# A graph network kernel: attention's software pipeline stretched, and its rings made longer

## The reference, cut to what matters

```python
h = relu(layernorm(x))
for l in range(3):                       # "the layers": mean over neighbours
    agg = segment_sum(h[src], dst) / degree
    h = leaky_relu(agg @ Wl.T + b + h @ Wr.T, 0.01)
x = x + h
h = relu(layernorm(x)) @ W               # "attention"
e = leaky_relu(a_s[src] + a_d[dst], 0.2) # with one more self edge per node
p = exp(e - segment_max(e, dst)[dst])
x = x + segment_sum(h[src] * p, dst) / segment_sum(p, dst) + bias
```

## Time and profile before

| | us |
|---|---|
| median of 3 runs (3214.66 to 3219.05) | 3217.39 |
| profiled execution | 3214.68 |
| its span | 3213.0 |
| PE busy | 2058.8 (64%) |
| DVE busy | 1978.0 (62%) |
| POOL busy | 1840.3 (57%) |
| ACT busy | 1405.6 (44%) |
| mean granted TensorE clock | 0.859 of 2.4 GHz |

### The profile page before, as it was taken

The page is one execution under the profiler, slowest core; times in us unless marked ns, Lnnn a source line. Parts: engine busy times, 40 slices in busy tenths (PEclk is TensorE's granted clock), DMA queues, the critical chain, the costliest instruction groups (busy, mean ns, idle before and its releaser), DMA issues. The chain is left out here.

```text
span 3213.0 us, 51338 instructions
## 1 busy us (share of the span) xinstructions
PE 2058.8 (64%) x12372; PEld 1794.7 (56%) x12372; DVE 1978.0 (62%) x8287; ACT 1405.6 (44%) x3735; POOL 1840.3 (57%) x1800
## 2 busy tenths in 40 slices
PE   0005877778765767777748888988944455445455
PEld 0004766666655656666647777877744444444444
DVE  8984444444444544444538888888846566666666
ACT  4781333333321222222215555555555555555555
POOL 1017666666646666666566666666535555555553
PEclk9997888889887988888869999999977777777778
DMA  6774766667655666666747777778745454445454
GB/s 210 254 254 122 201 194 192 192 191 199 189 161 152 203 194 197 192 190 198 209 127 223 221 225 224 220 220 225 219 124 129 123 128 125 125 124 130 124 129 113
DMA packets 600968, 576.10 MB, mean 179 GB/s; under 512 B 83395, under 2 KB 561301, under 8 KB 600640
## 3 DMA queue, kind: packets, MB, share of 16 engines
q1 hardware_dynamic: 402272, 337.58, 35.8%
q0 software_dynamic: 57280, 105.90, 14.9%
q10 hardware_dynamic: 141120, 129.32, 11.7%
HBM read 378.74 MB, written 207.75 MB: 183 GB/s over the span
## 5 line engine op out<-in xcount | busy, mean ns | idle before, releaser
L619 POOL DMA_INDIRECT rows<-tab,idx x1323 | 1373.2, 1038 | 808.0 <-issue 361.0
L834 PE MATMUL bank<-mask,rows 128*128 128x128 f32 (+1 forms) x3528 | 693.4, 336 | 176.8 <-issue 126.9
L1235 DVE TENSOR_TENSOR sage<-bank,sage 128x256 f32<-128x256 f32 x588 | 247.3, 421 | 835.7 <-remote 527.8
L834 PEld LDWEIGHTS bank<-mask,rows 128*128 128x128 f32 x3528 | 593.7, 211 | 248.0 <-issue 186.4
L619 POOL DMA_INDIRECT rows<-tab_c,idx x441 | 447.2, 1014 | 426.8 <-PE bank L945 177.2
L707 ACT ACTIVATE sage<-bank,b_col 128x256 f32<-128x256 f32 x392 | 185.2, 473 | 772.6 <-remote 462.5
L935 PE MATMUL bank<-ident,mask 128*128 128x128 f32 x784 | 168.5, 353 | 376.3 <-ACT mask L767 347.0
L1215 DVE TENSOR_SCALAR mask<-iota,dcol 128x256 f32<-128x256 f32 (+1 forms) x1323 | 406.2, 339 | 0.1
L935 PEld LDWEIGHTS bank<-ident,mask 128*128 128x128 f32 x784 | 121.6, 184 | 392.7 <-ACT mask L767 358.0
L787 ACT ACTIVATE sage<-cut_w,ed 128x256 f32<-128x256 bf16 (+1 forms) x441 | 184.8, 472 | 301.5 <-DVE ed L1439 289.5
L859 PE MATMUL bank<-sage,wcat 128*128 128x256 f32 x784 | 273.0, 434 | 43.1 <-issue 34.6
(11 more groups left out here) (210 smaller groups left out, 3402.6 us busy)
## 6 DMA issues: line engine op xcount, KB each, us to landing
sage<-inv_d SPq DMA_DIRECT2D x588, 128.0 KB
turned<-sage ACTq DMA_DIRECT2D x392, 128.0 KB
tab<-sage ACTq DMA_DIRECT2D x392, 128.0 KB
sage<-turned SPq DMA_DIRECT2D x392, 128.0 KB
tab_c<-sage ACTq DMA_DIRECT2D x196, 132.0 KB
own_w<-tab_c SPq DMA_DIRECT2D x196, 132.0 KB
tab<-sage SPq DMA_DIRECT2D x49, 512.0 KB, 3.6
xin<-tab SPq DMA_DIRECT2D x196, 128.0 KB
```

The lines of the kernel that those rows point to most:

```text
L619: eng.indirect_dma_start(out=rows[:, s.win[w], 0:width], out_offset=None, in_=table, in_offset=bass.IndirectOffsetOnAxis(ap=idx[:, s.w + w ...
L834: m = eng.matmul(to[:, a:b], rows[:, s.win[w], 0:D], mask[:, s.mw[w], c:c + b - a], start=(w == 1), stop=(w == 2))
L1235: eng.tensor_tensor(agg_t[:, o.r, :], ps[:, 0:TILE], own_t[:, o.v, :], ALU.add).then_inc(S["sum_v"], 1)
```

## The change

All rings counted in twelve tiles are counted in sixteen (`UNROLL`, `DEEP`): `rows` and `cut` hold 36 windows, `own_c` 16 tiles, `ed` and `pself_2` four groups. `DEEP` sets the waits of the gathers in all stages. In attention ACT takes the exponentials of tile s-7, PE the products of tile s-8, DVE the result of tile s-9, and DVE's back part runs two steps after the front part. The own rows' semaphores are one per group in place of one per tile, and DVE waits once per group. The space comes from the general path's tables, which now lie over `mask`.

```diff
-UNROLL = 12
+UNROLL = 16
-DEEP = 12
+DEEP = 16
...
-        low = sb("low", [P, P])
+        spare = mask[:, :, :].rearrange("p r e -> p (r e)")
+        low = spare[:, 0:128]
...
@@ sync, phase_c
-                        eng.dma_start(own_c[:, g.q, :, :], node_rows(tab_c, g.t)).then_inc(S[f"cl{g.q}"], 16)
+                        eng.dma_start(own_c[:, g.q, :, :], node_rows(tab_c, g.t)).then_inc(S[f"cl{g.g}"], 16)
@@ scalar, phase_c
-                o = s.at(-5)
+                o = s.at(-7)
...
-            steps(eng, 5, phase_c)
+            steps(eng, 7, phase_c)
@@ tensor, phase_c
-                o = s.at(-6)
+                o = s.at(-8)
...
-            steps(eng, 6, phase_c)
+            steps(eng, 8, phase_c)
@@ vector
         def fast_vector(eng, op, close_up):
+            eng.wait_ge(S["low_g"], 11)
...
                 if front:
-                    for n in range(SG):
-                        f = s.at(n - SG)
-                        eng.wait_ge(S[f"cl{f.q}"], 16 * (f.uses(DEEP) + 1))
+                    eng.wait_ge(S[f"cl{o.g}"], 16 * SG * (o.uses(DEEP) + 1))
...
-                r = s.at(-7)
+                r = s.at(-9)
...
-                b = s.at(-2)
-                back = b.there and s.k == 1
+                b = s.at(-3)
+                back = b.there and s.k == 2
...
-            steps(eng, 7, phase_c)
+            steps(eng, 9, phase_c)
```

More of the change, by code:

```diff
@@ L315, in build @@
         rden = sb("rden", [P, 2])
-        low = sb("low", [P, P])
+        spare = mask[:, :, :].rearrange("p r e -> p (r e)")
+        low = spare[:, 0:128]
         se = sb("se", [P, 2], I32)
[L320 to L325, removed]
+        g_row = spare[:, 128:260]
+        g_dst = spare[:, 260:392]
+        g_sum = spare[:, 392:524]
+        g_new = spare[:, 524:656]
+        g_node = spare[:, 656:788]
+        g_init = spare[:, 2068:2332].rearrange("p (j c) -> p j c", j=2)
         df = sb("df", [P, 1])
-        wide = sb("wide", [P, P])
-        same = sb("same", [P, P])
-        tmp = sb("tmp", [P, P])
+        wide = spare[:, 788:916]
+        same = spare[:, 916:1044]
+        tmp = spare[:, 1044:1172]
         g1 = sb("g1", [P, 8])
         w_idx = sb("w_idx", [P, 1], I32)
[L332 to L336, removed]
+        g_x = spare[:, 1172:1300]
+        g_x1 = spare[:, 1300:1428]
+        g_x1b = spare[:, 1428:1556]
+        g_h = spare[:, 1556:1684]
+        g_t = spare[:, 1684:1940]
         g_st = sb("g_st", [P, 6])
         g_mv = sb("g_mv", [P, 2])
-        g_out = sb("g_out", [P, D])
+        g_out = spare[:, 1940:2068]
         bank = [ctx.enter_context(nc.psum_tensor(f"bank{i}", [P, 512], F32)) for i in range(8)]
@@ L360, in build @@
                  "st3 x1_v x1b_v stx0 stx1 "
-                 "one_v turn cl0 cl1 cl2 cl3 cl4 cl5 cl6 cl7 cl8 cl9 cl10 cl11 cx0 cx1 cx2 cx3 cx4 cx5 cut_v sc_a zm_done "
+                 "one_v turn cl0 cl1 cl2 cl3 cx0 cx1 cx2 cx3 cx4 cx5 cut_v sc_a zm_done "
                  "mx_v mt_a fs_v pf_a br_done hs_v pr_a t1_v "
```

## The result

The changed kernel takes 3111.72 us, median of 4 runs (3110.88 to 3112.29), against 3218.12 us of the kernel before (4 runs, 3214.66 to 3219.05): a ratio of 0.9668, interval 0.9652 to 0.9684. The forecast was 3107. The profiled execution took 3110.88 us with a span of 3109.2, that is 103.8 us less than before.

A forecast was written before the change was run, and what follows sets the result against it. Attention was held by waits among ACT, DVE and PE, no engine full. From 3214.68 us, 42 x 2.33 = 97.9 and 7 x 2.28 = 16.0 off, 3 added: 3103.8; as a median 3106.5, say 3107, range 3060 to 3150 (chance 0.50).

The forecast's parts named there:

- Rings of sixteen: Gathers, all stages: deeper rings could win at most 43.6 us of PE's and the scores' waits; 0 taken for the layers.
- My own mark: Sign in the three layers: the prediction is wrong if they move by more than 15 us; within 5 us was expected.
- So if the lateness stays, DVE's 4.37 us stay, now at L1417: Attention, DVE's back part: the wait for PE moves from `edge_v` to the next mx, about 4 us a group.
- The ring of waits: Attention: ACT waits for `ed` of DVE (275.0 us), DVE at `edge_v` (163.1), PE for ACT's scores (330.0).
- another mark of mine: Sign in attention: wrong if DVE's mx at L1417 has no wait of about 4 us a group.
- my 14.6: Attention's mean group after the change: 42 groups at 15.13 us and 7 at POOL's floor of 11.7.
- a late group: Attention: one of 42 in 49 groups where DVE waits at L1413; 17.46 us before, 15.13 forecast, 2.33 saved each.
- The end: End of attention: two more tiles' results to make after the last score, about 3 us more, bounds 0 to 6.
- The lateness goes: Rival in attention: PE's late completions vanish or fall beside other work, POOL's 11.7 us is the floor; 2987 us, chance 0.29.
- The lateness grows with what is queued behind the bridge: Rival in attention: PE's release comes 2.5 us later, 17.63 us a group; 3253 us, slower, chance 0.12.
- No gain: Rival in attention: the wait moves whole to L1417, 17.46 us a group stays, 3 us added; 3220 us, chance 0.09.
- The rule on estimated ends: PE in attention: the profiler only estimates a matmul's end, so DVE's 4.37 us of idle time are PE's.

The follow-up runs named there:

- the first experiment: Changed kernel with the gathers of the three layers waiting as if the ring held twelve tiles, attention untouched: 3086.67 us, ratio 0.9596.
- the pipeline alone: Kernel before, rings of twelve kept, with only attention's steps moved to -7, -8, -9 and the back part to -3: 3095.3 us, ratio 0.9623.
- the leads (16, 12, 6): Changed kernel, layers' gathers waiting as for 16, 12 or 6 tiles: 3111.72 us, 3086.67 us; 6 in single layers: first 20 tiles 74.0 (layer 3), 62.0 us (layer 1).
- the pauses: Changed kernel with layers' lead 12, plus two waited-for POOL memsets after each of tiles 4 to 15 in attention: 2700.38 us on the other chip; first group 18.0 us in a mixed run.
- The additional raise: Changed kernel with layers' lead 12, plus one more PE semaphore raise per tile: 2675.27 us on the other chip; in mixed runs layer 1 662.4, layer 2 665.8 us.
- the last kernel: Changed kernel with layers' gathers waiting as for six tiles and attention's gathers also for the `mx` of the tile eight back: 3046.89 us, ratio 0.9477.

## Why the prediction was right in time and wrong in two steps

The time is 5 us from the forecast, and that is luck: by the table the layers and the first group took 36.7 us more than forecast, the other groups 29.2 us less. From the starts of the front parts, against what the sum had:

| part | forecast | measured |
|---|---|---|
| until attention's first front part (2378.19 to 2404.12) | 0 | +25.9 |
| first group (25.8 to 34.3) | -2.3 | +8.5 |
| the 46 groups behind it (779.9 to 643.7) | -106.9 | -136.1 |
| last interval and end | -1.6 | -2.1 |
| sum | -110.8 | -103.8 |

- **The step that failed: "Rings of sixteen ... I take 0 for the three layers (from -10 to +5)".** It cost 25.9 us, and the first experiment gave 25 us back by one number. I had read a deeper ring as room that can only help a waiting PE, and weighed the DMA engines as its one price. What I didn't read is that the ring's depth is the length of POOL's first run, and that PE's completions come late during it: nine gathers more a layer, 11.7 us. I read PE's waits for rows, of which the deeper ring won 6.5 us, and not DVE's for PE: L1235's 527.8 us on `remote` in the layers was the hint. My own mark, wrong if the layers move by more than 15 us, is met: in the layers the forecast was wrong.
- **"So if the lateness stays, DVE's 4.37 us stay, now at L1417".** Mis-sized. The ring of waits was broken as said (275 us at L787 gone, `edge_v` without a wait, scores no longer held), and PE's order does put mx behind the bridge. But the release isn't a fixed 5.95 us behind the bridge. It goes with where POOL's run ends, and with the changed waits the last gather before the release ends 1.98 us behind the last bridge matmul's start (median of the late groups) in place of 4.77, and 26 groups in place of 42 are late. The wait at L1418 is 45.6 us in all, under 1 us a group, where I had about 4, so another mark of mine (wrong if L1417 has no such wait) is as good as met; a result's wait at L1380 (90.1 us) took part of it. The mean group is 13.99 us in place of my 14.6 (42 x 15.13 and 7 x 11.7, over 49).
- **The first group** was counted as a late group. It is of another kind: POOL's run there is a whole ring.
- **The end** (+3) is small: last interval and end together gave -2.1 for -1.6. A small slip: the range from 3060 to 3150 is a saving of 1.4 to 3.2 us a group, not 1.2 to 3.1.
- **The rivals.** "The lateness goes" is what the other chip shows, 11.83 us a group against its 11.7; on the usual chip 13.99 is between it and the forecast. "The lateness grows with what is queued behind the bridge" forecast a release 2.3 us later; the late releases came 2.8 us sooner (3.12 for 5.95), and they go with what POOL issues beside the bridge. "No gain" fell by a group's 3.0 us. That the gain needed long rings fell with the pipeline alone.
- **The rule on estimated ends** (the Trainium skill, Perfetto Trace Analysis, Tensor Engine Instruction (MATMUL, LD_WEIGHTS)) held in the reading: in attention's first group the `mx` that reads the bank of transposes recorded until 2408.77 starts only at 2434.27, 25.5 us later. That this distance goes with POOL's gathers is this case's measurement.

**What stays open.** That long runs of gathers go with late completions of PE is shown by the leads (16, 12, 6), the pauses and the traces. What is held inside PE isn't: the matmuls themselves, their writes, or the reports of their end. The additional raise excludes only a cost per raise. Nor do the runs separate POOL's issuing from the gathers' traffic in the DMA engines, as leads and pauses change both. Nor is it shown why one chip has none of it with the same gathers. I did not run the pipeline alone with short leads, which may be faster than the last kernel.

## What to carry to other kernels

A prefetch ring's depth is also the length of the burst at each stage's start: look at what that burst does to the other engines before deepening it, and limit the lead to what the consumer needs. Where a release comes long after the recorded end, lay the other engines' timelines beside it and look for the event that it follows by a constant distance, as 1.2 us behind POOL's last gather here. Split a change that bundles a longer pipeline with larger buffers; here one part brought all of the gain, and the other took some 15 of its 121 us back (0.9623 against 0.9668).

## What the runs showed of the hardware

- On the chips where the kernel before takes some 3215 us, completions of PE during back-to-back indirect gathers come late and few: DVE stood idle up to 28.2 us before one sum of the layers and 22.85 us before one `mx`, and 1.2 to 4 us after the run's end the pending ones came together. The loss isn't in PE's busy time nor in the granted clock, which is 0.01 lower at most in the layers.
- One chip shows none of it, with gathers of the same 1.00 us at the same 1.30 us spacing: the kernel before takes 2711.96 us there, 16% less. A change to gathers or rings has to be judged on both kinds: the changed kernel's variants are 4 to 5% faster on the one and 0.4 to 1.4% on the other, where the change itself was not run.
- Memsets on POOL with waits between the gathers relieve PE at once (attention's first group 18.0 us in place of 35.7, with the same gathers); so what matters is how closely the gathers follow each other, not their number.
